# A four-layer gated transformer kernel: causal attention's end with row sums spread by products and the inverse on ScalarE, unread products added, quantised feed-forward shared out anew

## The reference

```
# layer 0, cross attention: 16 heads of 8;   layer 3's is the same without biases
scores = q k^T / sqrt(8);  out = softmax(scores) v
# layer 0, feed-forward
h   = layernorm(x) * gamma + beta
h   = gelu(qlinear(h, w1, b1));  out = qlinear(h, w2, b2)
# qlinear: sx = 127 / max|row|;  xq = round(x * sx);  y = xq wq / (sx * sw) + b
# layer 1, cross attention, second half: 16 heads of 32 over the context
# layer 1, feed-forward: starts with a causal attention of 16 heads of 8
att = where(tril, q k^T, 0) / sqrt(128)       # later keys keep the score 0
out = softmax(att) v                          # ... and so a share each
# then each token goes to one of 8 experts, layernorm
```

## Time and profile before

| | us |
|---|---|
| median of 3 runs | 1822.11 |
| lowest, highest of them | 1819.84, 1838.12 |
| profiled execution | 1825.63 |
| its span | 1823.9 |

### The profile page before, as it was taken

How to read it: one execution, slowest core, us unless ns; L and a number is a source line. 1 busy time by engine, 2 the same in 40 slices (tenths; PEclk the granted TensorE clock), 3 DMA queues, 4 the chain that set the end, 5 groups by cost and what they waited for, 6 DMA issues and landing times.

```text
span 1823.9 us, 21924 instructions
## 1 busy us (share of the span) xinstructions
PE 1560.7 (86%) x8770; PEld 706.0 (39%) x8772; DVE 873.3 (48%) x1690; ACT 734.3 (40%) x1295; POOL 148.6 (8%) x209
## 2 busy tenths in 40 slices
PE   4848999798899989978669999888999989888296
PEld 2223333342444436523133323333444437533284
DVE  4364786333665352334555774433664442436212
ACT  2444555424454134242344555243453144252043
POOL 0000112000021000000000112000011000002321
PEclk9869999999998689886678999899997789899698
DMA  4000000000000100000000000000000100030241
GB/s 191 1 1 0 1 1 1 0 1 1 0 2 1 47 0 1 1 2 1 1 1 1 1 1 1 0 1 0 1 2 1 47 0 1 1 80 1 72 140 60
DMA packets 18105, 30.27 MB, mean 17 GB/s; under 512 B 4640, under 2 KB 12640, under 8 KB 17104
## 3 DMA queue, kind: packets, MB, share of 16 engines
q1 hardware_dynamic: 16752, 26.23, 4.6%
q0 software_dynamic: 1248, 2.59, 0.4%
HBM read 23.62 MB, written 5.19 MB: 16 GB/s over the span
## 4 chain that ended last, share of the span: by engine, by line
PE 77%; DVE 12%; ACT 7%; issue 2%; DMA 1%; POOL 1%; SPq 0%; POOLq 0%; DVEq 0%; ACTq 0%
PE ps L820 7%; PE ps L927 5%; PE ps L701 4%; PE ps L866 3%; PE ps L646 3%; PE ps L1377 3%; PE ps L1389 3%; PE ps L1057 3%; PE ps L740 3%; PE ps L978 3%; PE ps L958 2%; PE ps L1065 2%; PE ps L879 2%; PE ps L678 2%; PE ps L1292 2%
## 5 line engine op out<-in xcount | busy, mean ns | idle before, releaser
L2061 DVE TENSOR_REDUCE peak<-ps 128x1 f32<-128x512 f32 x256 | 163.3, 682 | 94.6 <-PE ps L820 94.5
L1692 ACT ACTIVATE big<-ps 128x512 f32<-128x512 f32 x256 | 138.4, 596 | 113.2 <-PE ps L858 112.4
L820 PE MATMUL ps<-pp,qT 32*128 32x512 f32 x512 | 147.9, 661 | 1.4 <-ACT pp L1798 1.4
L849 PE MATMUL ps<-qT,pp 32*128 32x512 f32 x512 | 148.2, 654 | 0.0
L1715 ACT ACTIVATE big<-ps 128x512 f32<-128x512 f32 (+3 forms) x256 | 101.2, 437 | 116.8 <-PE ps L958 115.9
L2106 DVE TENSOR_REDUCE crest<-ps 128x2 f32<-128x512 f32 (+3 forms) x128 | 104.9, 824 | 61.7 <-PE ps L933 61.5
L958 PE MATMUL ps<-qT,pp 32*128 32x384 f32 (+3 forms) x512 | 130.8, 521 | 2.3 <-ACT big L1715 1.4
L1631 ACT ACTIVATE big<-ps 77x1024 f32<-77x1024 f32 x96 | 93.5, 1016 | 92.7 <-PE ps L701 92.3
L2002 DVE TENSOR_REDUCE small<-ps 128x8 f32<-128x616 f32 x96 | 74.3, 797 | 95.1 <-PE ps L674 57.4
L927 PE MATMUL ps<-pp,qT 32*128 32x384 f32 (+3 forms) x512 | 105.4, 480 | 5.3 <-DVE crest L2106 2.7
L1611 ACT ACTIVATE sq<-ps 128x512 f32<-128x512 f32 x48 | 28.7, 597 | 187.5 <-PE ps L646 187.5
(11 more groups left out here) (480 smaller groups left out, 2720.1 us busy)
## 6 DMA issues: line engine op xcount, KB each, us to landing
big<-in_w SPq DMA_DIRECT2D x23, 256.0 KB, 3.3
pt<-in_l2w SPq DMA_DIRECT2D x2, 2048.0 KB, 7.6
w_l<-in_l SPq DMA_DIRECT2D x1, 3086.0 KB, 18.0
pp<-in_w SPq DMA_DIRECT2D x1, 2048.0 KB, 10.3
big<-by_expert SPq DMA_DIRECT2D x23, 66.0 KB, 2.0
by_expert<-cst SPq DMA_DIRECT2D x1, 1472.0 KB, 17.1
cst<-in_const SPq DMA_DIRECT2D x1, 1427.0 KB, 7.0
w_l<-in_l SPq DMA_DIRECT2D x1, 1218.0 KB, 9.1
```

The source lines that it names most:

```text
L820: pe.matmul(rbank(x), qT[at, u, k, 128 * i:128 * i + 128], keyT(u, k)[at, :], start=True, stop=True, tile_position=(32 * c, 0)).then_inc(* ...
L849: pe.matmul(a1_bank(y), keyT(u, k)[at, 128 * j:128 * j + 128], qT[at, u, k, :], start=True, stop=False, tile_position=(32 * c, 0))
L1692: A(prob(m)[:, TURN_OF[g], :], a1_bank(tplace(m, g)), ACT.Exp).then_inc(*SCALAR.did("a1", "exp", m, g))
L2061: v.tensor_reduce(peak[:, p // 4 % 2, i, c:c + 1], rbank(ring(p, c)), AX.X, ALU.max)\
```

## The change

It joins three edits. (1) In the causal attention's end `shares(u)` takes the place of `heads(u, 0)`, `heads(u, 1)` and `spread_out("inv", u)`: two products with `swapped` of 512 columns and four with the later keys' counts (`counted`, which VectorE now writes eightfold) accumulate the sums in the values' rows, and ScalarE takes logarithm and exponential over 128 x 512 (`inverse`), for `u` = 0 behind block 28, for `u` = 1 behind the first copy of the routing's one-hot table. VectorE's add, reciprocal and eightfold copy go. (2) `unread` multiplies the identity with `w1q` into a bank that nobody reads: in `cross` between the row scores, around `turned(0)` and behind `turned(1)`, and two in each of the steps 26 to 31 of the causal attention. (3) In the quantised feed-forward ScalarE takes over the second sequence's normalisation, the first one's copy of the turned values and its second rounding, VectorE takes over the second sequence's copies of turned values, and the second product of the first sequence is issued between the transposes of the second.

```diff
+            def unread(bank, n):
+                for _ in range(n):
+                    pe.matmul(bank, identb[:], w1q[:], start=True, stop=True)
...
                 for a in range(8):
+                    if a and dh == 8:
+                        unread(PSB[0], 1)
                     rowscores(0, a)
+                unread(PSB[0], 3)
                 turned(0)
+                unread(PSB[0], 2)
...
                 turned(1)
+                if dh == 8:
+                    pe.wait_ge(*SCALAR[tag, "kept", 0, 0])
+                    unread(PSB[0], 2)
...
+                def shares(u):
+                    bank = PSB[(4, 7)[u]]
+                    pe.wait_ge(*VECTOR["l1f", "e0 rest", u])
+                    if u:
+                        pe.wait_ge(*SCALAR["l1f", "exp", 31, 3])
+                    for hf in (0, 1):
+                        pe.wait_ge(*SCALAR["l1f", "kept", 2 * u + hf])
+                        pe.matmul(bank, K["swapped"][:, 128 * hf:128 * hf + 128], kept_sums(2 * u + hf), start=hf == 0, stop=False,
+                                  skip_group_check=True)
                     for i in range(4):
+                        mm = pe.matmul(bank[:, 128 * i:128 * i + 128], counted(u)[:, 128 * i:128 * i + 128], ident, start=False,
+                                       stop=True, skip_group_check=True)
+                    mm.then_inc(*TENSOR.did("l1f", "shares", u))
...
                         spread_out("e0", 0, 1)
-                        heads(0, 0)
-                        heads(0, 1)
-                    if m == 29:
-                        spread_out("inv", 0, 4)
+                        shares(0)
                     if m == 30:
                         spread_out("e0", 1, 2)
                     if m == 31:
                         logits(0)
+                    if 26 <= m < 32:
+                        unread(PSB[2 if m < 28 else 3], 2)
...
                 turned_hot(0)
-                heads(1, 0)
-                heads(1, 1)
+                past_shares(1)
...
-                    if n == 1:
-                        spread_out("inv", 1, 7)
...
+            def inverse(u):
+                act.wait_ge(*TENSOR["l1f", "shares", u])
+                A(x2[:, u, :], PSB[(4, 7)[u]], ACT.Ln).then_inc(*SCALAR.did("l1f", "log", u))
+                act.wait_ge(*SCALAR["l1f", "log", u])
+                A(x2[:, u, :], x2[:, u, :], ACT.Exp, scale=-1.0).then_inc(*SCALAR.did("l1f", "inv", u))
...
+                act.wait_ge(*VECTOR["l0f inverse", 60, 0])
+                for i in range(4):
+                    ins = A(hid[0][:, i, :], hid[0][:, i, :], ACT.Identity, bias=K["magic"], scale=sm(0, 64 + i, 1))
...
+                pe.wait_ge(*VECTOR["l0f q2", 1])
+                for i in range(4):
+                    pe.wait_ge(*SCALAR["l0f xq2", 0, i])
+                    turned2(1, i)
+                    second(0, i)
+                for i in range(4):
+                    pe.wait_ge(*VECTOR["l0f xq2", 1, i])
+                    second(1, i)
```

More of the change, by code:

```diff
@@ L70, in const_table @@
     t["unmagic"] = np.full((128, 1), -MAGIC, f)
+    t["magic"] = np.full((128, 1), MAGIC, f)
     t["rowid"] = i[:, None].astype(f)
@@ L325, in kept_sums, with counted @@
             return (part if r % 2 == 0 else rs)[:, r // 2, :]
+        def counted(u):
+            return (xn[:, 1, :], part[:, 0, :])[u]
         TURN_OF = (2, 3, 0, 1)
@@ L1777, in _ @@
                 token_rstd("l0f a")
+                act.wait_ge(*VECTOR["l0f a", "offset"])
+                for i in range(4):
+                    ins = A(xn[:, 1, 128 * i:128 * i + 128], aux(1)[:, 128 * i:128 * i + 128], ACT.Identity,
+                            bias=sm(1, 40 + i, 1), scale=sm(1, 44 + i, 1))
+                ins.then_inc(*SCALAR.did("l0f a", "n", 1))
                 act.wait_ge(*VECTOR["l0f rounded", 50, 0])
@@ L2157, in gathered_values @@
                                            ALU.add).then_inc(*VECTOR.did("l1f", "o", r))
-                def inverse(u):
-                    total = sm(u, 0, 64)
-                    v.wait_ge(*VECTOR["l1f", "e0 sum", u])
-                    v.wait_ge(*TENSOR["l1f", "heads", u, 1])
-                    chain(v.tensor_tensor(total, PSB[(2, 7)[u]][:, 0:64], sm(u, 128, 64), ALU.add))
-                    chain(v.reciprocal(total, total))
-                    v.wait_ge(*TENSOR["l1f", "e0", u])
-                    v.tensor_copy(by_eight(u), eightfold(total)).then_inc(*VECTOR.did("l1f", "inv", u))
                 def divided(u):
-                    v.wait_ge(*TENSOR["l1f", "inv", u])
+                    v.wait_ge(*SCALAR["l1f", "inv", u])
                     v.wait_ge(*VECTOR["l1f", "o", 2 * u + 1])
-                    chain(v.tensor_tensor(sq[:, u, :], sq[:, u, :], PSB[(4, 7)[u]], ALU.mult))
+                    chain(v.tensor_tensor(sq[:, u, :], sq[:, u, :], x2[:, u, :], ALU.mult))
                     v.tensor_scalar(x2[:, u, :], sq[:, u, :], W["l1f"]["bv"], None, ALU.add)\
@@ L2195, in attend_past @@
                 gathered_values(3)
-                inverse(1)
                 only_of(2)
@@ L2258, in quantise @@
                 v.tensor_scalar(am, am, mw, 1.0 / 127.0, ALU.mult, ALU.mult).then_inc(*VECTOR.did())
+                VECTOR.table["l0f inverse", at, u] = VECTOR.n
+                if at == 60 and u == 0:
+                    return
                 v.wait_ge(*VECTOR.last())
@@ L2333, in _ @@
                     quantise("l0f q2", u, hid[u], tq2(u).rearrange("p (i f) -> p i f", i=4), wabs[:, 1:2], 60)
+                for i in range(4):
+                    v.wait_ge(*TENSOR["l0f q2T", 1, i])
+                    v.tensor_copy(xq2(1)[:, :, 128 * i:128 * i + 128],
+                                  scb(i).bitcast(BF16)[:, 0:512].rearrange("p (c s) -> p c s", c=4))\
+                        .then_inc(*VECTOR.did("l0f xq2", 1, i))
                 for u in U:
```

102 lines of the change are left out of this document (49 added, 53 removed).

## The result

The changed kernel takes 1772.54 us (median of 4 runs, 1770.68 to 1774.03), the kernel before 1821.38 on the same chip: ratio 0.9689, 95% interval [0.9632, 0.9747]. That is 48.9 us less; 41 were forecast (1780). The profiled execution took 1774.03 us, 51.6 less than that of before; its span is 1772.3, its mean clock 0.921 where it was 0.882. Executions of the kernel before spread from 1800.99 to 1841.11 us on one chip, and a profile shows one execution of its kernel.

A forecast was written before the change was run, and what follows sets the result against it. TensorE, on the last-ending chain for 77% and partly at half clock, was taken as the bound. Crosses 18, causal attention's end 20 and feed-forward 4 make 42 off 1825.6, less 3.5 for the median: 1780 us, range 1763 to 1801.

The forecast's parts named there:

- The crosses: Cross attentions: unread products hold TensorE's clock at full behind the row scores, 18 us won, two thirds of 26.7.
- Between the row scores they are free: Cross attentions' row scores: unread products there cost nothing, as TensorE waits for VectorE's maxima.
- a gap bridged by 1.1 us of products: Cross attentions, 3.2 us gap around the first transposes: five unread products, 1.1 us, hold the clock in most places.
- In most places and not in all: Cross attentions: the bridged gap keeps full clock mostly, since falls are partly chance; hence 18 of 26.7 us.
- the bound of 26.7: Crosses, a2 included: the most the unread products can give back if the clock holds everywhere, 26.7 us.
- The causal attention's end: Steps 26 to 31 through the third expert: wide sums and unread products at full clock win 10 us a turn, 20.
- a second fall: Rival: clock falls again at step 28 or 29 as ScalarE stalls column scores; 10 us in both turns, 1790; chance 0.13.
- the wide sums put 3.2 us of full-array products: Causal attention's end: argument against the slower case, full-array products standing where those of 8 columns stood.
- The feed-forward: Quantised feed-forward: moving work between VectorE and ScalarE wins 2 us a turn, 4 in all.
- its four pieces take as long as VectorE's did: Feed-forward: ScalarE's rounding takes VectorE's time, 1.68 us, so the first sequence's transposes stay at about 113.66.
- The gap's fall: Rival: clock falls behind the crosses' row scores in most of six places; crosses give 6, not 18: 1792; chance 0.17.
- The slower case: Rival: clock falls where it fell and unread products are paid on TensorE's path, 16 us less 4: 1834; chance 0.04.

## Why the prediction was right, point by point

*The crosses.* In sum 17.3 us, and 1.7 around a2, where 18 was forecast: luck, by a division that was wrong on both sides. Behind the first column score the four crosses won 25.6 us, all of their part of the bound and more (31.4 us each, where 32 to 33 were the sign to look for), and ahead of it they lost 8.3. "Between the row scores they are free" failed: the seven took 2.1 us in each of four crosses, as the step went from VectorE's pace to TensorE's. The mechanism, "a gap bridged by 1.1 us of products", failed too, for the fall doesn't come from the gap: the earlier trace rows show the clock at 0.50 from 41.75 and from 772.20 on, 0.20 and 0.01 us behind the last row score, and in turn 2 of layer 0, as in 22 of the 24 crosses without the seven, it falls while row scores still run. The work in the gap brings it back, and the seven that were counted as free are what keeps it. "In most places and not in all" failed the other way: of the 36 crosses of the nine kernels with work in the gap none was caught, and eight lost 1.3 us. And the bound of 26.7, taken from one execution, isn't a fixed loss: it stands for how many crosses happened to be caught there.

*The causal attention's end.* 10 us a turn were forecast, with 5 more in the experts as a bound; 11.6 and 5.6 came, so 34.4 us in both turns where 20 were counted. That is the term that was too small, and what was not foreseen (below) took 4.8 back. By its steps, read in the timeline of the kernel after:

```profile
577.39 1.02 PE L1007 MATMUL ps<-part,cst 128*128 128x512 f32 x2
...
583.02 1.13 PE L975 MATMUL ps<-qT,pp 32*128 32x512 f32 x4
...
597.71 0.39 PE L1294 MATMUL ps<-identb,small 128*8 128x128 bf16 x4 [0.17 <-DVE small L2476]
...
601.03 0.82 PE L1311 MATMUL ps<-xn,identb 8*128 8x512 bf16 x3
...
604.93 1.13 PE L1317 MATMUL ps<-big,w_l1f 128*128 128x512 f32 x2
```

```profile
586.77 0.60 ACT L1753 ACTIVATE x<-ps 128x512 f32<-128x512 f32 x1
587.41 0.63 ACT L1755 ACTIVATE x<-x 128x512 f32<-128x512 f32 x1
```

From step 28 to the routing's transposes 14.7 us (15.0 forecast), the sum for `u` = 1 3.3 (4.0), then to the end of the third expert 5.0 (5). ScalarE's logarithm and exponential take 0.60 and 0.63, as estimated. Step 29, where a second fall was feared, held. What the step "the wide sums put 3.2 us of full-array products" got wrong is the agent: the wide sums at least halve the stretch at half clock, the unread products alone remove it.

*The feed-forward.* 2 us a turn forecast, 1.4 and 2.9 measured, 2.7 as the mean of six turns with the edit (36.5) against six without (39.2). The step "its four pieces take as long as VectorE's did" failed, without harm. Timeline of the kernel after, answering:

```profile
105.38 2.93 ACT L1824 ACTIVATE big<-big,cst,small 128x512 f32<-128x512 f32 x4
...
110.40 2.31 PE L1188 MATMUL ps<-identb,qT 128*128 128x128 bf16 x20 [10.46 <-ACT qT L1827]
```

ScalarE's rounding takes 2.93 us where VectorE's took 1.68. The normalisation that was won ahead of it pays for that: the transposes begin 28.7 us behind the stage's first, 28.6 before.

*What was not foreseen.* The start of the causal attention took 26.4 us before and takes 28.7 now. Windows, before and then after:

```profile
473.85:500.20 26.35, 24.83 (x150) 12.49 (x150) 16.47 (x31) 10.73 (x20) 1.07 (x2) 0.94 0.00 1
```

```profile
471.51:500.20 28.69, 27.56 (x151) 13.35 (x151) 16.63 (x31) 10.75 (x20) 1.08 (x2) 0.82 0.00 1
```

No edit is there. All seven kernels with work in a2's gap and nothing at this place have 28.7 to 28.8 in both turns; of the ten turns without, nine have 26.4 and one 28.9. So something upstream decides where the narrow row scores lose the clock; in the kernel with one product in each of the first pairs of row scores the start took 25.7. How the place is decided stays open. But it takes back what a2's products win: from a2's first row score to the causal attention's first value product the ten turns without them take 127.7 to 131.5 us (129.3 in both turns of before), the fourteen with them 129.7 to 131.9 (129.7 in twelve). So the 2.7 us that the prediction counted for a2 didn't last.

*The rivals.* The gap's fall didn't come in the changed kernel, and its ground, that transposes count for nothing, was shown wrong. A second fall didn't come. The slower case needs a clock that stays at 0.50 with the products paid for: nowhere seen, but the kernel without any of them, 1841, shows how far the crosses can go.

## What to carry to other kernels

Where TensorE bounds a stage of narrow products and has lost its clock ahead of it, put full-array work that nobody reads into the gap before the stage: five products were worth up to 17 us in a cross (57.2 against 39.9). Narrow work in that gap wasn't tried. Where a narrow stage has no gap, as in the causal attention's end, two such products in each step kept the clock. Between tiles that overlap they cost more than their own time: seven, 7 x 0.22 = 1.5 us, cost 2.1. Ahead of an engine's drain 20 that took 4.5 us cost 3.0. Read the clock where it falls and where it comes back, and not only its mean behind the gap. Where a loss comes and goes with edits elsewhere, compare kernels by stages: two of these edits were worth 5 and 34 us in their stages while the totals showed nothing and 21.

## What the runs showed of the hardware

A TensorE that is busy 44.43 of 47.77 us by its records can be at 0.50 all the time, in a stage where most products use 32 rows or 32 columns of the array. That isn't the only case: in the experts of the kernel before it is busy all of 10.23 us at 0.50, about seven of them with products on the full array. Transposes brought the clock back in a gap as products of the same columns did: 24 of them, with no product, stand in the 3.09 us at 0.50 before it rose. Twelve products on 32 rows each took 1.31 us together, and four 0.79 once a full-array product stood between the groups.
